# Attention gates of the first two row blocks as bf16 parts, made by GpSimd and VectorE, in a fused attention and routed-mixture kernel

## The chip, the cores and the metric

The kernel runs on one core of one Trainium2 chip. The metric is device time in microseconds (us), and smaller is better. Three runs of the kernel before took 287.94, 531.36 and 285.32 us, with a median of 287.94 us. The execution that the profiler recorded took 286.6 us; its span, from the first instruction to the last, is 284.8 us.

## The reference

The input x has 8 sequences of 512 rows of 256 numbers. A first layer computes causal attention scores of the rotated projections q and k; for every row it keeps only one number, the sum of the exponentials, `o`. That number goes through a tiny two-layer network, the **gate**: `relu(o * fc1_w + fc1_b)` has 16 values, and `fc2_w` (256 x 16) with `fc2_b` turns them into 256. The result is added to x and normalised to x1.

A second layer is a top-3 mixture of 12 experts:

```
xa = x1 @ P_w.T
C1, C2, C3 = top-3 softmax weights of xa @ U1.T, xa @ U2.T, xa @ U3.T
h  = gelu(sum_e C1[:, e] * (x1 @ W1[e].T))
y  = sum_e C2[:, e] * (h @ W2[e].T) + C3 @ b2
out = layernorm(x1 + y)
```

## The kernel before, in words

**Tiling.** The 4096 rows are 32 tiles of 128 rows. A tile mixes 16 rows of each of the 8 sequences. Four tiles are a group, so there are 8 groups (0 to 7); two groups are one block T of 128 positions, so there are 4 blocks. The attention is done in 8 chunks c = 0 to 7; chunk c holds block T = c // 2 of four sequences. Groups 2T and 2T+1 need the sums of block T.

**Three stages.** (1) The chunk loop: for each chunk, TensorE makes four fp32 projections (`project`, line 914), ScalarE copies each out of PSUM (`qk_copy`), VectorE rotates them (`rope`, lines 1279 and 1285), TensorE makes the scores and ScalarE the exponentials (`exps`). Work for the first groups is mixed in by hand through `early_aux`: the gate's product `fc`, its addition to x (`fc_add`), the statistics (`norm_stats`), scale and shift of the norm (`norm_scale`, on GpSimd), the normalised rows (`normed`, on ScalarE), their transposes and the router. (2) A middle part written out by hand: tile 0 goes through all 12 experts, tiles 1 to 3 through the chosen ones. (3) The steady loop over i = 4 to 33: first mixture of tile i, second mixture of tile i-2.

**Weights.** The expert weights are split into two fp16 parts. ScalarE and VectorE split the first experts (`w_high`, `w_low`). GpSimd splits the other 16 in 16 pieces (`w_piece`: lines 464, 466, 467), one after the other, from chunk 4 on. The first piece waits for the scales of the weights (`scale_done`) and for `fc2_spread`, the copies of the gate's second weight matrix, since it overwrites the buffer `wtmp` from which they are made. Between pieces GpSimd runs `norm_scale(0)` (before piece 0), `norm_scale(1)` (before piece 5), and the routing weights (`chosen_exps`, `weights_of`; before piece 9). Behind piece 14 comes `bias_add(0, 0)` (line 500), for which the second mixture of tile 0 waits.

**Gates.** For blocks 0 and 1, TensorE spreads `o` over 32 partitions with an fp32 transpose (`gate_spread`, after chunks 1 to 4), ScalarE applies scale, bias and relu (`gate_relu`), and `fc` is an fp32 product. For blocks 2 and 3, GpSimd computes the gate with rows on partitions and cuts it into six bf16 parts (`gate_parts`, seven linked operations), TensorE transposes them (`gate_transpose`), ScalarE copies them (`gate_copy`), and `fc` is a bf16 product against `fc2s`, the six stacked copies of the weights (`fc2_spread`, six transfers issued on the SP queue in chunk 5, each followed by one for b2).

**Order.** Each engine runs its list strictly in the order written. Buffers: two PSUM banks for projections, four for expert products, one (`ROWS`) for gate and bias rows, one (`XPOSE`) shared by the transposes of x1, C3 and the gates.

## Time and profile before

| | us |
|---|---|
| profiled execution | 286.6 |
| its span | 284.8 |
| TensorE busy in the span | 259.5 (91%) |
| VectorE busy | 214.8 (75%) |
| GpSimd busy | 180.3 (63%) |
| ScalarE busy | 175.0 (61%) |
| runs, median of 3 | 287.94 |

The shares are averages over three stages with different limits. The chunk loop takes up to about 84 us, the middle part up to about 130 us, the steady loop the rest. Which engine sets the pace has to be read stage by stage, in the chain of waits.

### The profile page before, as it was taken

What the parts mean: (1) busy time and instruction counts of PE and PEld (TensorE: products, weight loads), DVE (VectorE), ACT (ScalarE), POOL (GpSimd) and SP (SyncE); (2) the same over time, 40 slices, a digit from 0 to 9 for tenths busy, and PEclk for the clock granted to TensorE, in tenths of its full rate; (3) what the DMA queues carried; (4) which work ended last, traced back from release to release, by engine and by line L of the source; (5) the groups of instructions that cost most, each with busy time, mean ns of one, the idle gap of its engine ahead of it and who ended that gap; (6) DMA issues with size and microseconds to landing.
All of it is one profiled execution on the core that took longest, in us unless ns stands there. A gap on an engine that the chain in (4) does not pass through costs nothing.

```text
span 284.8 us, 6483 instructions
## 1 busy us (share of the span) xinstructions
PE 259.5 (91%) x2016; PEld 191.6 (67%) x2016; DVE 214.8 (75%) x668; ACT 175.0 (61%) x376; POOL 180.3 (63%) x367
## 2 busy tenths in 40 slices
PE   7999999997997878799899998998998999999980
PEld 5444455453455666678688897897897898887960
DVE  0359869779969938848898899899897877765671
ACT  2235966665763632816958957867878858655541
POOL 2640005999989998727785775685774864855552
PEclk9999999999999999959999999999999999999997
DMA  7999994997000000000001001001011010100112
GB/s 226 393 380 359 155 213 73 211 136 92 0 3 0 0 3 0 0 21 1 22 22 33 26 20 39 21 20 41 18 32 29 18 39 18 41 20 24 36 37 60
DMA packets 19546, 20.51 MB, mean 72 GB/s; under 512 B 1643, under 2 KB 18870, under 8 KB 18998
## 3 DMA queue, kind: packets, MB, share of 16 engines
q1 hardware_dynamic: 18518, 19.14, 28.4%
q10 hardware_dynamic: 992, 0.93, 1.1%
q8 instruction: 18, 0.29, 0.5%
q14 instruction: 18, 0.15, 0.2%
HBM read 15.78 MB, written 4.19 MB: 70 GB/s over the span
## 4 chain that ended last, share of the span: by engine, by line
PE 48%; POOL 20%; ACT 8%; DVE 7%; issue 6%; SPq 5%; DMA 3%; POOLq 0%; DVEq 0%; ACTq 0%
PE bank L1110 33%; PE bank L914 8%; POOL W L467 7%; POOL wtmp L464 5%; POOL W L466 4%; DVE early L1526 3%; DMA early<-in_xT 2%; PE bank L1190 2%; SPq L372 2%; ACT early L723 2%; SPq L400 1%; SPq L367 1%; PE bank L989 1%; ACT L702 1%; SPq L399 1%
## 5 line engine op out<-in xcount | busy, mean ns | idle before, releaser
L1110 PE MATMUL bank<-W,early 128*128 (+1 forms) x630 | 77.2, 277 | 4.8 <-ACT early L780 1.8
L1110 PE MATMUL bank<-W,x1T 128*128 (+1 forms) x630 | 75.0, 273 | 4.0 <-issue 2.1
L1110 PEld LDWEIGHTS bank<-W,early 128*128 128x128 f16 x630 | 61.4, 99 | 15.0 <-ACT early L780 2.6
L1110 PEld LDWEIGHTS bank<-W,x1T 128*128 128x128 f16 x630 | 60.3, 98 | 13.8 <-issue 4.5
L914 PE MATMUL bank<-early,wqk 128*128 128x512 f32 x128 | 60.3, 602 | 1.0 <-DMA early<-in_xT 1.0
L1526 DVE SCALAR_TENSOR_TENSOR early<-bank,Csel,early 128x256 f32<-128x256 f32 x95 | 45.7, 482 | 15.3 <-ACT early L780 5.4
L588 POOL TENSOR_TENSOR early<-early 128x256 f32<-128x256 f32 x29 | 21.0, 725 | 30.8 <-DVE early L1526 28.2
L658 ACT ACTIVATE qk<-bank 128x512 bf16<-128x512 f32 x32 | 19.0, 595 | 31.3 <-PE bank L914 31.2
L914 PEld LDWEIGHTS bank<-early,wqk 128*128 128x128 f32 x128 | 22.3, 190 | 21.2 <-issue 20.5
L785 ACT ACTIVATE early<-early 128x256 f32<-128x256 f32 x32 | 13.3, 417 | 35.1 <-DVE early L1526 35.0
L1279 DVE TENSOR_TENSOR xturn<-qk,turn 128x2048 bf16<-128x2048 bf16 x16 | 21.1, 1320 | 15.9 <-ACT qk L658 15.9
L1526 DVE SCALAR_TENSOR_TENSOR early<-bank,Csel,xs 128x256 f32<-128x256 f32 x31 | 14.8, 479 | 11.5 <-PE bank L1110 10.9
L827 ACT ACTIVATE early<-bank,ipow 128x256 f16<-128x256 f32 x32 | 15.0, 469 | 10.8 <-PE bank L1190 10.7
L840 ACT ACTIVATE early<-early,shift,rstd 128x256 f32<-128x256 f32 x32 | 18.8, 588 | 4.4 <-POOL shift L596 4.4
L467 POOL TENSOR_TENSOR W<-wtmp,W 128x512 f16<-128x512 f32 x16 | 20.3, 1269 | 1.4
L710 ACT ACTIVATE x<-xs,shift,rstd 128x256 f32<-128x256 f32 x32 | 17.4, 594 | 5.9 <-POOL shift L495 5.8
L492 POOL TENSOR_SCALAR ve<-mv 128x4 f32<-128x4 f32 x8 | 2.8, 352 | 28.0 <-DVE mv L1359 27.5
L500 POOL TENSOR_TENSOR xs<-early,x 128x512 f32<-128x512 f32 x16 | 20.3, 1269 | 0.0
L595 POOL TENSOR_TENSOR rstd<-ve,minus_half 128x1 f32<-128x1 f32 x32 | 18.0, 561 | 2.7
L666 ACT ACTIVATE expd<-bank 128x128 bf16<-128x128 f32 (+3 forms) x32 | 13.6, 435 | 8.4 <-PE bank L929 8.4
L1566 DVE SCALAR_TENSOR_TENSOR early<-bank,ipow,early 128x256 f16<-128x256 f32 x32 | 14.6, 457 | 5.1 <-ACT early L827 5.0
L464 POOL TENSOR_SCALAR wtmp<-W,scale 128x512 f32<-128x512 f32 x16 | 16.2, 1014 | 1.7 <-DMA fc2s<-wtmp 1.7
(139 smaller groups left out, 453.7 us busy)
## 6 DMA issues: line engine op xcount, KB each, us to landing
early<-in_xT SPq DMA_DIRECT2D x16, 256.0 KB, 7.4
xs<-in_x SPq DMA_DIRECT2D x32, 128.0 KB, 7.4
out<-early SPq DMA_DIRECT2D x32, 128.0 KB
W<-in_w1T SPq DMA_DIRECT2D x1, 2048.0 KB, 12.2
W<-in_w2T SPq DMA_DIRECT2D x1, 2048.0 KB, 12.9
W<-in_w1T SPq DMA_DIRECT2D x1, 1024.0 KB, 7.7
W<-in_w2T SPq DMA_DIRECT2D x1, 1024.0 KB, 14.6
wqk<-in_wqkT ACTq DMA_DIRECT2D x1, 512.0 KB, 3.7
```

Of the source, the lines that this page charges most:

```text
L464: link(pool.tensor_scalar(wtmp[:, n % 2, :], Wf[:, WS * m + e + 2, :], scale[:, 1 + m:2 + m], 0.0, ALU.mult, ALU.add))
L467: pool.tensor_tensor(W[:, m, e + 1, 1, :], wtmp[:, n % 2, :], W[:, m, e + 1, 0, :], ALU.subtract)\
L500: pool.tensor_tensor(xs[:, t:t + 2, :].rearrange("p t d -> p (t d)"), brows[:, h, :], x1[:, g % 3, 2 * h:2 * h + 2, :].rearrange("p t d -> ...
L588: pool.tensor_tensor(y[:, t % 4, :], y[:, t % 4, :], part[:, t % 2, :], ALU.add).then_inc(late_added, 1)
L595: link(pool.tensor_tensor(rstd2[:, p:p + 1], ve2[:, p:p + 1], minus_half[:, 0:1], ALU.pow))
L658: act.activation(qk[:, c % 2, g, :, :].rearrange("p s n -> p (s n)"), bank[PROJ[n % 2]][:, :], ACT.Copy)\
L710: n = act.activation(x1[:, g % 3, t, :], xs[:, GT * g + t, :], ACT.Identity, bias=shift[:, g % 2, t:t + 1], scale=rstd[:, g % 2, t:t + 1])
L840: act.activation(y[:, t % 4, :], y[:, t % 4, :], ACT.Identity, bias=shift2[:, p:p + 1], scale=rstd2[:, p:p + 1]).then_inc(y_done, 1)
L914: mm = pe.matmul(bank[PROJ[n % 2]][:, :], wqk[:, k, g, :], xTb[:, c % 4, k, :, :].rearrange("p s n -> p (s n)"), start=(k == 0), stop=(k = ...
L1110: mm = pe.matmul(where[:, 0:DIM], lhs(hx, c), w, start=(k == 0), stop=(k == 5))
L1279: link(dve.tensor_tensor(xturn[:, :, :, :, :], src, turns, ALU.mult))
L1526: dve.scalar_tensor_tensor(sums, bank[place[n]][:, 0:DIM], c, before, ALU.mult, ALU.add)\
```

## The change

Blocks 0 and 1 get their gates in six bf16 parts as well. Block 0's parts are made by GpSimd in chunk 2 and block 1's by VectorE at the head of chunk 5. `gate_spread`, `gate_relu`, the fp32 matrix `fc2w` and its transfer go. `fc2s` is spread in chunk 4, ahead of chunk 5's load. In chunk 3 the steps of the first gate product and its addition move to after the transposes of the weights' maxima, on TensorE and VectorE. `norm_scale(0)` moves behind piece 0 of the weights; the split of C3 and the selection for group 0 move from chunk 7 to chunk 6. In the middle part a product of tile 1 and an addition change places, and the second mixture of tile 0 takes its first four experts in the opposite order. In the steady loop the expert numbers are loaded earlier, and of the first mixture of a group's first tile one or two products (three for group 1) stand between the two bias products. Small changes of buffers and semaphores are left out.

```diff
--- before.py
+++ after.py
...
@@ -326,6 +320,10 @@
+        def dense_expert(m, j):
+            return NB - 1 - j if m and j < NB else j
@@ -386,13 +384,12 @@
             load_chunk(3)
-            sp.dma_start(fc2w[:, :], fc2[0:2 * PAD, :]).then_inc(ld_fc2, 16)
             load_rows(0)
                     load_rows(c // 2 - 1)
-                if c == 5:
+                if c == 4:
                     sp.wait_ge(fc2_split, 1)
@@ -471,8 +468,8 @@
                 pool.wait_ge(exp_done, NSEQ * (T + 1))
-                wait(pool, hgT_done, T - 2)
-                if T == 2:
+                wait(pool, hgT_done, T)
+                if T == 0:
                     pool.wait_ge(gwb_done, 1)
@@ -565,20 +562,21 @@
                         continue
-                    if (c, j) == (3, 3):
+                    if (c, j) == (2, 3):
+                        gate_parts(0)
+                    if (c, j) == (4, 1):
                         norm_scale(0)
                         weights_of(0)
+                    if (c, j) == (6, 2):
+                        C3_split(0)
+                        select_of(0)
                     if c >= 4:
                         piece += 1
-                    if (c, j) == (NCH - 1, 0):
-                        C3_split(0)
-                    if (c, j) == (NCH - 1, 2):
-                        select_of(0)
             bias_add(0, 0)
@@ -675,16 +673,9 @@
-            def gate_relu(c):
-                T, b = c // 2, SPC * (c % 2)
-                act.wait_ge(gate_done, c + 1)
-                act.activation(hgf[PAD * T:PAD * (T + 1), :, b:b + SPC, :].rearrange("p u s r -> p s u r"),
-                               bank[HGT][0:PAD, :].rearrange("p (s u r) -> p s u r", s=SPC, r=RPS), ACT.Relu,
-                               bias=gatew[0:PAD, 1:2], scale=gatew[0:PAD, 0:1]).then_inc(gate_copied, 1)
             def gate_copy(T):
-                act.wait_ge(hgT_done, T - 1)
-                act.activation(hgT[0:NP * NI, T - 2, :, :, :].rearrange("p u s r -> p s u r"),
+                act.wait_ge(hgT_done, T + 1)
+                act.activation(hgT[0:NP * NI, T, :, :, :].rearrange("p u s r -> p s u r"),
                                bank[XPOSE][0:NP * NI, :].bitcast(BF16).rearrange("p (s u r) -> p s u r", s=NSEQ, r=RPS),
@@ -747,15 +738,15 @@
                     normed(3, 0)
-                if (s, pos) == (0, 1):
-                    if group(k):
-                        bias_copy(k, 0)
+                if (s, pos) == (0, 1) and group(k):
+                    bias_copy(k, 0)
                     if k == 1:
-                        final(1)
+                        begin(GT)
                     if routed(k + 1):
                         exp_route(k + 1)
-                    if group(k):
-                        bias_copy(k, 1)
+                    if k > 1:
+                        begin(GT * k)
+                    bias_copy(k, 1)
                 if (s, pos) == (1, 1):
@@ -802,13 +793,13 @@
                 qk_copy(c, 2)
+                if c in (3, 6):
+                    gate_copy(c // 6)
                 if c:
                 qk_copy(c, 3)
-                if 1 <= c <= 4:
-                    gate_relu(c - 1)
                 early_aux(c, 2, early)
@@ -842,10 +833,10 @@
             begin(0)
+            exps(NCH - 1, 0)
             w_high(NB + 2)
-            exps(NCH - 1, 0)
+            exps(NCH - 1, 1)
             w_high(NB + 3)
-            exps(NCH - 1, 1)
             gelu(0)
@@ -876,8 +867,11 @@
                 if i < NT:
-                    begin(i)
+                    if s:
+                        begin(i)
                     gelu(i)
+                if i == GT:
+                    final(1)
                 if late(i - 3):
@@ -929,19 +923,10 @@
-            def gate_spread(c):
-                T, b = c // 2, SPC * (c % 2)
-                pe.wait_ge(exp_done, SPC * (c + 1))
-                wait(pe, gate_copied, c)
-                for s in range(SPC):
-                    tr = pe.transpose(bank[HGT][0:PAD, P * s:P * (s + 1)],
-                                      o[:, T, b + s:b + s + 1].to_broadcast([P, PAD]), identf[:, :])
-                tr.then_inc(gate_done, 1)
             def gate_transpose(T):
-                pe.wait_ge(hgp_done, T - 1)
+                pe.wait_ge(hgp_done, T + 1)
                 wait(pe, hgT_copied, begun["gate"])
-                pe.wait_ge(x1lo_done, begun["x1T"])
+                wait(pe, x1lo_done, begun["x1T"])
                 wait(pe, C3T_copied, begun["C3T"])
@@ -972,21 +957,16 @@
                 if g == 0 and h == 0:
-                    pe.wait_ge(ld_fc2, 16)
-                if T == 2 and g % 2 == 0 and h == 0:
                     pe.wait_ge(fc2_spread, 16 * NP)
-                if h == 0 and T < 2:
-                    pe.wait_ge(gate_copied, 2 * (T + 1))
-                if h == 0 and T >= 2:
-                    pe.wait_ge(hgT_copied, T - 1)
+                if h == 0:
+                    pe.wait_ge(hgT_copied, T + 1)
                 wait(pe, bias_copied, begun["bias"])
                     u = (GT * g + t) % 8
-                    lhs, rhs = (hgf[PAD * T:PAD * (T + 1), u, :, :], fc2w[PAD * T:PAD * (T + 1), :]) if T < 2 else \
-                        (hgT[0:NP * NI, T - 2, u, :, :], fc2s[:, :])
-                    mm = pe.matmul(bank[ROWS][:, t % 2 * DIM:(t % 2 + 1) * DIM], lhs.rearrange("p b r -> p (b r)"), rhs,
+                    mm = pe.matmul(bank[ROWS][:, t % 2 * DIM:(t % 2 + 1) * DIM],
+                                   hgT[0:NP * NI, T, u, :, :].rearrange("p b r -> p (b r)"), fc2s[:, :],
                                    start=True, stop=True)
@@ -1059,7 +1039,7 @@
                         x1_transpose(k + 1, 1)
-                if (s, pos) == (1, 0) and group(k + 1):
+                if (s, pos) == (1, 1) and group(k + 1):
                     route_logits(k + 1)
@@ -1075,11 +1055,12 @@
                         bias(k, 0)
-                    if between(k):
-                        routed_first(GT * k)
-                    if later(k + 2):
-                        x1_transpose(k + 2, 0)
-                    if group(k):
+                        if k == 1:
+                            routed_first(GT, range(TOPK))
+                        if later(k + 2):
+                            x1_transpose(k + 2, 0)
+                        if k > 1:
+                            routed_first(GT * k, range(ahead(k)))
                         bias(k, 1)
@@ -1095,8 +1076,8 @@
-            def between(k):
-                return k in (1, NG - 2, NG - 1)
+            def ahead(k):
+                return TOPK if k == 1 else 1 if later(k + 2) else 2
@@ -1117,7 +1098,7 @@
                         pe.wait_ge(acc_begun if act else slot_added, count)
-                    e = j + 1 if t == 0 else held_ids[t // GT][REC * m + j]
+                    e = dense_expert(m, j) + 1 if t == 0 else held_ids[t // GT][REC * m + j]
                     products(bank[place[n]], lhs, m, e).then_inc(slot_done, 1)
@@ -1136,8 +1117,11 @@
                     gate_rows()
-                early_aux(c, 0, early)
+                if c != 3:
+                    early_aux(c, 0, early)
                 project(c, 1)
+                if c == 3:
+                    gate_transpose(0)
                 if c == 0:
@@ -1148,20 +1132,22 @@
                 project(c, 2)
-                early_aux(c, 2, early)
+                if c != 3:
+                    early_aux(c, 2, early)
+                if c == 6:
+                    gate_transpose(1)
                 if c == NCH - 1:
                 if c == 3:
-                    pe.wait_ge(gwb_done, 1)
                     peak_transpose()
+                    early_aux(c, 0, early)
                 project(c, 3)
                     peak_spread()
+                    early_aux(c, 2, early)
                 early_aux(c, 3, early)
-                if 1 <= c <= 4:
-                    gate_spread(c - 1)
@@ -1175,8 +1161,7 @@
             first(range(4, 6))
-            pe.wait_ge(gate_copied, 4)
-            pe.wait_ge(ids_done, 1)
+            load_ids(0)
             scores(NCH - 1, 0)
@@ -1194,10 +1179,8 @@
-            def routed_first(t):
-                if t % GT == 0 or t == 1:
-                    load_ids(t // GT)
-                mixture(t, 0, lambda hx, c: x1T[:, t, hx, c, :], range(TOPK))
+            def routed_first(t, js=range(TOPK)):
+                mixture(t, 0, lambda hx, c: x1T[:, t, hx, c, :], js)
@@ -1205,8 +1188,10 @@
             route_logits(1)
+            pe.wait_ge(wlo_done, NM * NB - 1)
+            second(0, range(0, NB - 1))
             pe.wait_ge(wlo_done, NM * NB)
-            second(0, range(0, NB))
+            second(0, range(NB - 1, NB))
             pe.wait_ge(w_split, NM * (NE - NB) - 2)
@@ -1217,10 +1202,11 @@
             fc(3, 0)
+            gate_transpose(2)
             route_count(1)
-            gate_transpose(2)
+            second(1, range(0, 1))
             fc(3, 1)
-            second(1, range(TOPK))
+            second(1, range(1, TOPK))
             h_transpose(2)
@@ -1230,11 +1216,13 @@
                 second(i - 2, range(TOPK))
+                if s == 0 and i < NT:
+                    load_ids(k)
                 if i <= NT:
                 aux(k, s, 1)
-                if i < NT and (s or not between(k)):
-                    routed_first(i)
+                if i < NT:
+                    routed_first(i, range(0 if s else ahead(k), TOPK))
@@ -1269,6 +1257,21 @@
+            def gate_parts(T):
+                dve.wait_ge(exp_done, NSEQ * (T + 1))
+                dve.wait_ge(hgT_done, T)
+                w, b = (gwb[:, n, :].unsqueeze(1).to_broadcast([P, NSEQ, NI]) for n in range(2))
+                f = hg[:, :, :].unsqueeze(2)
+                link(dve.tensor_tensor(hg[:, :, :], o[:, T, :].unsqueeze(2).to_broadcast([P, NSEQ, NI]), w, ALU.mult))
+                link(dve.tensor_tensor(hg[:, :, :], hg[:, :, :], b, ALU.add))
+                link(dve.tensor_scalar(hg[:, :, :], hg[:, :, :], 0.0, None, ALU.max))
+                link(dve.tensor_copy(hgp[:, :, 0:3, :], f.to_broadcast([P, NSEQ, 3, NI])))
+                link(dve.tensor_tensor(hg[:, :, :], hg[:, :, :], hgp[:, :, 0, :], ALU.subtract))
+                link(dve.tensor_copy(hgp[:, :, 3:5, :], f.to_broadcast([P, NSEQ, 2, NI])))
+                dve.tensor_tensor(hgp[:, :, 5, :], hg[:, :, :], hgp[:, :, 3, :], ALU.subtract).then_inc(hgp_done, 1)
...
@@ -1486,8 +1490,11 @@
             for c in range(NCH):
+                if c == 5:
+                    gate_parts(1)
                 early_aux(c, 0, early)
-                early_aux(c, 1, early)
+                if c != 3:
+                    early_aux(c, 1, early)
                 if c == 4:
@@ -1505,11 +1512,11 @@
                     peak_pow()
+                    early_aux(c, 1, early)
                 if c in (4, 5):
                 if c == NCH - 1:
-                    w_low(NB + 1)
                     break
@@ -1520,7 +1527,7 @@
                 n = slot[t, m, j]
-                e = j + 1
+                e = dense_expert(m, j) + 1
                 c = C[:, 0, m, e:e + 1] if t == 0 else Csel[:, t, m, j:j + 1]
@@ -1572,14 +1579,15 @@
             first_mixture(0, (4,))
-            w_low(NB + 2)
+            w_low(NB + 1)
             first_mixture(0, (5,))
             first_mixture(0, (6, 7))
-            w_low(NB + 3)
+            w_low(NB + 2)
             fc_add(2, 1)
             norm_stats(2)
+            w_low(NB + 3)
             h_low(0)
@@ -1591,9 +1599,9 @@
             route_mask(1)
+            fc_add(3, 0)
             first_mixture(2)
             route_sums(1)
-            fc_add(3, 0)
             route_ids(1)
```

## Rows read from the trace of the kernel before

**Rows 1.** The chain of waits, 49 to 108 us: start, us, what ended last.
```profile
49.28 0.90 POOL wtmp L464
...
106.10 1.24 POOL xs L500
107.36 0.49 DVE early L1526
```
**Rows 2.** Windows: us, busy of PE, PEld, DVE, ACT, POOL; granted clock, DMA share, GB/s.
```profile
67.30:84.70 17.40, 17.10 (x69) 7.97 (x66) 14.59 (x56) 11.39 (x30) 15.87 (x19) 1.00 0.10 13
...
160.00:200.00 40.00, 38.29 (x390) 33.38 (x388) 36.16 (x140) 30.24 (x64) 27.24 (x71) 1.00 0.10 28
```
**Rows 3.** The timeline of the SP queue: start, us, issue, tensors, count.
```profile
16.93 6.96 SPq L389 DMA_DIRECT2D fc2w<-in_fc  x1
27.87 1.94 SPq L367 DMA_DIRECT2D early<-in_xT  x2
39.66 0.71 SPq L399 DMA_DIRECT2D fc2s<-wtmp  x1
```
**Rows 4.** The timeline of GpSimd: start, us, line, operation [idle before, releaser].
```profile
52.43 1.67 POOL L464 TENSOR_SCALAR wtmp<-W,scale 128x512 f32<-128x512 f32 x1
...
66.13 0.24 POOL L492 TENSOR_SCALAR ve<-mv 128x4 f32<-128x4 f32 x1
...
109.99 0.23 POOL L492 TENSOR_SCALAR ve<-mv 128x4 f32<-128x4 f32 x1
...
111.72 0.20 POOL L495 TENSOR_TENSOR shift<-shift,rstd 128x4 f32<-128x4 f32 x1
```
**Rows 5.** The timeline of VectorE, 46 to 66 us.
```profile
46.75 0.17 DVE L1319 TENSOR_SCALAR scale<-ipow 128x3 f32<-128x3 f32 x1
...
51.81 1.73 DVE L1279 TENSOR_TENSOR xturn<-qk,turn 128x2048 bf16<-128x2048 bf16 x1 [1.06 <-ACT qk L658]
...
58.80 0.69 DVE L1367 TENSOR_TENSOR x1T<-bank,x1T 128x512 f16<-128x512 f32 x1 [2.55 <-ACT x1T L717]
...
65.64 0.38 DVE L1359 BATCH_NORM_AGGREGATE mv<-stats 128x2 f32<-128x6 f32 x4
```
**Rows 6.** The timelines of ScalarE and TensorE, 47 to 52 us.
```profile
47.74 1.10 ACT L710 ACTIVATE x<-xs,shift,rstd 128x256 f32<-128x256 f32 x2
...
50.98 0.60 PE L1001 MATMUL bank<-identf,x 128*128 128x128 f32 x4
...
51.85 1.88 PE L914 MATMUL bank<-early,wqk 128*128 128x512 f32 x4
```
**Rows 7.** Instructions by source line: ns min/median/max, first and last start in us.
```profile
L1383 DVE TENSOR_TENSOR dz<-zs,top x8: 308/309/1059, 70.7 to 239.4; 128x144 f32<-128x144 f32 x8
...
L989 PE MATMUL bank<-fc2w,hgf x32: 374/374/762, 33.3 to 122.3; 32*128 32x256 f32 x32
...
L989 PE MATMUL bank<-fc2s,hgT x16: 270/274/283, 129.8 to 203.2; 102*128 102x256 bf16 x16
```
**Rows 8.** Windows of 1 us, columns as in Rows 2.
```profile
118.00:119.00 1.00, 0.48 (x7) 0.14 (x5) 1.00 (x4) 1.00 (x1) 0.35 (x2) 1.00 0.00 0
...
121.00:122.00 1.00, 1.00 (x3) 0.81 (x4) 0.93 (x5) 0.53 (x2) 0.79 (x4) 0.50 0.00 0
```
**Rows 9.** The timeline of TensorE, 120 to 127 us.
```profile
120.84 2.04 PE L989 MATMUL bank<-fc2w,hgf 32*128 32x256 f32 x4 [1.20 <-DVE xs L1349]
122.82 4.02 PE L1110 MATMUL bank<-W,early 128*128 x18
```
**Rows 10.** The timelines of TensorE and ScalarE at the start of group 2.
```profile
157.21 2.15 PE L1110 MATMUL bank<-W,x1T 128*128 x18 [0.40 <-issue]
...
161.17 0.38 PE L1190 MATMUL bank<-identf,early 128*128 128x128 f32 x2
...
160.09 0.42 ACT L785 ACTIVATE early<-early 128x256 f32<-128x256 f32 x1
```
**Rows 11.** Waits of TensorE, 123 to 284 us: total, times, longest.
```profile
PE bank L1110 <- ACT early L780: 1.8, 3, 0.9
```

10 lines of the change are left out of this document (3 added, 7 removed).

## The prediction

> **What bounds the kernel now.** I read the chain of waits first, then the windows, then the timelines of single engines. From 49.28 to 107.36 us the chain lies on GpSimd: the 16 pieces of the weights, with other work between them, then the addition of bias rows (line 500), for which VectorE's first sum of the second mixture waits [rows 1]. Beside it TensorE is nearly full in the loop (17.10 of 17.40 us), but it doesn't end last there [rows 2]. In the steady loop TensorE sets the pace (38.29 of 40 us), with VectorE close behind (36.16) [rows 2]. So a microsecond saved on TensorE counts after about 107 us; before, only what moves GpSimd's chain counts. The profiled execution took 286.6 us, its span 284.8; the sum below is made against these. The median shown is 287.94, 0.5% more. About 2%, 5.7 us, is what a measurement of this kernel tells from no change.
>
> **Gate products and spreads, in the loop.** An fp32 product call is four matmuls of 0.374 us at least in the record, a bf16 one two of 0.274 [rows 7]; they overlap, and from start to next start the calls cost about 1.1 and 0.3, so 0.8 is saved per call. Six of the eight calls lie before 107 us. They, the four spreads and the four relus are worth nothing: GpSimd's chain covers them. If that cover were gone they would be worth 5 us.
>
> **The weight copies for the gate, earlier on SP.** The six transfers (and six for b2) now follow chunk 4's load, whose issue ends at 29.8 us, and the first product waits for all six. Before, from the first issue (39.66) to the start of piece 0, which waited for them (49.28), took 9.6 us [rows 1, 3]. From 29.8 that gives 39.4. They are issued behind a full queue, as the transfer for the old fp32 weights was, which held SP for 6.96 us [rows 3]; so they may land up to 7 us later. I take 40.5, nearer to the first row, which is the same transfer. Chunk 5's load moves behind 12 issues and still has 10 us to land before 51.85 [rows 6]: nothing. Block 0's parts on GpSimd lie in an idle stretch: nothing.
>
> **Scales 1.7 us later.** The first additions move behind the maxima, and the second product now stands behind the fourth projection of chunk 3. VectorE's addition, statistics and rotation stand ahead of the scales, so they end at 48.6 us and not at 46.92 [rows 5]. I estimate 1.7, one fp32 projection (line 914: 1.88 for four matmuls [rows 6]) less slack; the bounds are 0 and 3.
>
> **First norm behind piece 0.** Piece 0 can't begin before the scales: 48.6. It took 3.15 (49.28 to 52.43) [rows 1, 4], so it ends at 51.8. `norm_scale(0)` takes 1.93 with VectorE quiet (109.99 to 111.92) [rows 4], so it ends at 53.7. ScalarE began the normalised rows at 47.74 [rows 6]: now 53.7, and in its list everything waits behind them: a weight split, the copies of projections 2 and 3, more exponentials. TensorE's transposes start at 54.8 instead of 50.98 [rows 6], chunk 5's projections about 4 us late. Of SP nothing waits. The last copy of chunk 4 ends at 57.3, so VectorE's rotation starts at 57.4 instead of 51.81 [rows 5]: **+5.6**. GpSimd itself loses nothing yet.
>
> **Block 1's parts on VectorE.** Seven linked operations at the head of chunk 5. The nearest row is a fp32 operation on 128x144: 0.309 alone, 1.059 once, at 70.7 us, beside the pieces [rows 7]. Lower bound 7 x 0.31 = 2.2; upper 7 x 1.06 plus links = 7.7. I take 5.5: four operations with two tensor inputs at 1.06, three with one at 0.31, and links. VectorE had 2.55 idle there, waiting for ScalarE [rows 5]; the late rotation makes it the last, so this idle time goes. Its statistics for group 1 ended at 66.02 [rows 5]: 66.0 + 5.6 + 5.5 - 2.55 = 74.6, less 1.5, since GpSimd by then stands and no longer slows VectorE: 73.1.
>
> **GpSimd's chain: +6.7.** `norm_scale(1)` began at 66.13, just after these statistics [rows 4], and eleven pieces are queued behind it. It begins at 73.2 and takes 1.93 where it took 2.4. Line 500 moves by 6.7. Bounds: 2.5 (scales on time, piece 0 at its shortest, the parts 2.2) and 9.
>
> **The early split of C3 and selection, expert order, early numbers: nothing** before 107 us. They let TensorE reach the second mixture at about 104, where it makes four products and stops: its four banks are full, and VectorE waits for line 500 until 114. **Clock: +2.0.** In the profile TensorE, busy 0.48 us of the microsecond from 118, had a granted clock of 0.50 (1.2 of 2.4 GHz) at 121 [rows 8], and 18 matmuls took 4.02 us against 2.15 [rows 9, 10]: 0.6 per expert. The new idle stretch is over 4 us; three or four experts run slow. Bounds 0 and 3.4.
>
> **The middle part behind it: -4.9.** The fp32 calls of group 3: 0.8 off the first; the wait of 1.20 for VectorE's addition goes (that addition is earlier, and a product of tile 1 fills in); the second call shrinks from 1.98 to 0.2; 18 matmuls at full clock give 1.9 [rows 9, 10]. That is 5.7; I take off 0.8 for VectorE, which then ends last. Bounds 3 and 6.
>
> **Group boundaries.** ScalarE's first product copy comes before a table load or a bias copy; TensorE waited three times for it, 1.8 in all [rows 11]: **-1.8**. In groups 2 to 5 a product fills the wait between the bias products, and the numbers are loaded early; 0.40 of the idle time there is the loading [rows 10]. But the transposes of h can't start before the gelu's end at 160.5; they started at 161.17 [rows 10]. So 0.67 each: **-2.7**. Bounds 0 and -4.7.
>
> **Sum:** 6.7 + 2.0 - 4.9 - 1.8 - 2.7 = -0.7; 286.6 - 0.7 = 285.9 us.
>
> **Rivals.** *A, the forecast:* 285.9, its own range 282.5 to 289; chance 0.40.
>
> *B, the early loss is small:* the rotation catches up, the parts take 2.2, the clock holds. 2.5 - 4.9 - 1.8 - 2.7 = -6.9: 279.7. For it: VectorE waits 2.55 in that stretch. Against it: ScalarE's list is strict. Chance 0.22.
>
> *C, slower, the weight copies in a full queue:* if their last part lands later than about 42 us, TensorE stands in front of the first gate product, with projection, scales and pieces behind it. With 5 us lost there (the hold of 6.96 less 2 of slack): 285.9 + 5 = 290.9. For it: the hold [rows 3]. Against it: the copies were issued 0.7 apart behind eight loads. Chance 0.13.
>
> *D, the boundaries give nothing,* since VectorE, busy 36.16 of 40, becomes the bound [rows 2]: 285.9 + 4.5 = 290.4. Chance 0.15.
>
> *E, every operation of block 1's parts waits for a whole operation of a piece:* 7.7 us instead of 5.5, and 2.2 more on the chain: 288.1. The row at 1.06 against 0.31 speaks for it, rotations beside pieces, 1.73 against 1.2, only mildly [rows 5, 7]. Chance 0.10. The Trainium skill, page "SBUF — State Buffer", section "SBUF: two separate sides", states this as an exclusive lock between VectorE and GpSimd, held for the whole instruction, the other fully blocked. By that rule the trace's 1.06 would be the normal case for all seven.
>
> **Range and chances.** From 279 to 291: it takes in B, C, D and E. The part of B below 280.9 is most of it: faster by over 2%, 0.22. C and D together, or a stall of TensorE in chunk 4 that also halves its clock among the fp32 projections, would pass 292.3: slower by over 2%, 0.10. The rest, 0.68, is within 2%.
>
> **What would show it.** Piece 0 starting before `norm_scale(0)`, the copies at line 710 starting at 53 to 54, idle TensorE before its first transposes; block 1's seven operations at about 0.7 us each, and GpSimd idle before its second `norm_scale` (right for A; no idle there means B). Line 500 at 112 to 114, then a clock of 0.50. The stretch from the first sum of the second mixture to tile 3's first product (107.4 to 127.8 before) about 3 us shorter. Group boundaries 0.7 shorter. I am wrong if TensorE stands before the first gate product for over 2 us (C), or if line 500 comes before 109 (B).

## The result: a little slower, where no change was forecast

The changed kernel took 289.4 us (median of 4 runs, 289.1 to 291.0): a ratio of 1.014 to the kernel before, 95% interval 1.009 to 1.019. Beside it the kernel before took 285.1, 285.3 and 287.9; a fourth run, 531.4, was slow and is left out; it is in the median of 287.94 that the opening gives. The profiled execution took 289.3 us, its span 287.4, against 286.6 and 284.8 before. The forecast was 285.9, 0.7 less than 286.6; the span grew by 2.6. The time lies inside the range, but the sign was wrong by more than the interval.

The page of the changed kernel: the span, the busy time of each engine, TensorE's granted clock in 40 slices.
```profile
span 287.4 us, 6466 instructions
...
PE 252.3 (88%) x2000; PEld 188.3 (66%) x2000; DVE 219.3 (76%) x675; ACT 173.0 (60%) x374; POOL 183.4 (64%) x374
...
PEclk9999999979999999599999999999999999999996
```
TensorE has 7.2 us less to do than before and the span is 2.6 us longer: most of what went was covered, the waits that came were not. The row PEclk is the clock that TensorE was granted, in tenths of full speed. By windows of 1 us it was halved (0.50) from 57.6 to 60.7 us and from 115.6 to 122.1 us; the last digit is the end, where TensorE has nothing left. "To stand" below means that an engine waits.

The chain of waits of the changed kernel answers to [rows 1] (start, us, what ended last; "issue" is time without a wait that shows):
```profile
49.53 0.71 POOL wtmp L461
...
53.87 1.06 POOL rstd L490
55.53 1.09 ACT x L701 x2
...
58.96 1.32 DVE xturn L1282
...
64.33 1.36 DVE hgp L1270
...
75.03 1.05 POOL rstd L490
...
114.95 1.23 POOL xs L497
116.83 2.72 PE bank L1091 x12
```
Before, one engine carried this stretch. Now the chain leaves GpSimd behind piece 0, goes over ScalarE and VectorE, through block 1's parts (line 1270), and comes back at 75 us. Lines 461 to 464 are the pieces, 497 the addition of bias rows.

The timelines of the same kernel, GpSimd and then VectorE, TensorE and the copies, answer to [rows 4, 5, 6]; in brackets stands the idle time ahead and what ended it:
```profile
49.53 0.70 POOL L461 TENSOR_SCALAR wtmp<-W,scale 128x512 f32<-128x512 f32 x1 [14.33 <-DVE scale L1322]
...
53.23 0.56 POOL L489 TENSOR_SCALAR ve<-mv 128x4 f32<-128x4 f32 x1
...
62.28 1.26 POOL L461 TENSOR_SCALAR wtmp<-W,scale 128x512 f32<-128x512 f32 x1
63.60 0.61 POOL L463 CAST W<-wtmp 128x512 f16<-128x512 f32 x1
64.30 1.16 POOL L464 TENSOR_TENSOR W<-wtmp,W 128x512 f16<-128x512 f32 x1
65.43 0.81 POOL L461 TENSOR_SCALAR wtmp<-W,scale 128x512 f32<-128x512 f32 x1
66.31 0.61 POOL L463 CAST W<-wtmp 128x512 f16<-128x512 f32 x1
67.00 1.15 POOL L464 TENSOR_TENSOR W<-wtmp,W 128x512 f16<-128x512 f32 x1
74.70 0.24 POOL L489 TENSOR_SCALAR ve<-mv 128x4 f32<-128x4 f32 x1 [6.55 <-DVE mv L1363]
...
114.91 1.26 POOL L497 TENSOR_TENSOR xs<-early,x 128x512 f32<-128x512 f32 x1
```
```profile
49.19 0.17 DVE L1322 TENSOR_SCALAR scale<-ipow 128x3 f32<-128x3 f32 x1
...
55.53 1.09 ACT L701 ACTIVATE x<-xs,shift,rstd 128x256 f32<-128x256 f32 x2 [5.72 <-POOL shift L492]
...
56.68 0.66 PE L981 MATMUL bank<-identf,x 128*128 128x128 f32 x4 [3.37 <-ACT x L701]
57.86 3.35 PE L908 MATMUL bank<-early,wqk 128*128 128x512 f32 x4 [0.53 <-ACT qk L656]
...
58.96 1.31 DVE L1282 TENSOR_TENSOR xturn<-qk,turn 128x2048 bf16<-128x2048 bf16 x1 [0.33 <-ACT qk L656]
...
62.77 0.29 DVE L1267 TENSOR_TENSOR hg<-o,gwb 128x136 f32<-128x136 f32 x1
63.09 0.59 DVE L1268 TENSOR_TENSOR hg<-hg,gwb 128x136 f32<-128x136 f32 x1
63.71 0.58 DVE L1269 TENSOR_SCALAR hg<-hg 128x136 f32<-128x136 f32 x1
64.33 1.35 DVE L1270 CAST hgp<-hg 128x408 bf16<-128x408 f32 x1
65.72 0.67 DVE L1271 TENSOR_TENSOR hg<-hg,hgp 128x136 f32<-128x136 f32 x1
66.42 0.65 DVE L1272 CAST hgp<-hg 128x272 bf16<-128x272 f32 x1
67.11 1.20 DVE L1273 TENSOR_TENSOR hgp<-hg,hgp 128x136 bf16<-128x136 f32 x1
...
68.97 0.39 PE L968 MATMUL bank<-fc2s,hgT 102*128 102x256 bf16 x2 [3.28 <-DVE xs L1353]
```
Lay the two side by side: from 63.1 on each of the last six of block 1's seven operations ends 0.1 to 0.2 us after the GpSimd operation that had started before it: 63.68 after 63.54, 64.29 after 64.21, 65.68 after 65.46, 66.39 after 66.24, 67.07 after 66.92, 68.31 after 68.15. Their ends follow GpSimd's; e3 below has the same operations where they need not wait. The first of the seven (62.77) took 0.29; there GpSimd's operation took long, 1.26 for what takes 0.69 at its shortest, so there GpSimd seems to have been the one that waited.

And TensorE's first gate product, then its stand in front of the fifth product of tile 0's second mixture:
```profile
41.27 0.39 PE L968 MATMUL bank<-fc2s,hgT 102*128 102x256 bf16 x2 [2.39 <-DMA fc2s<-wtmp]
...
116.83 2.72 PE L1091 MATMUL bank<-W,early 128*128 128x256 f16 x12 [5.40 <-DVE early L1533]
...
125.51 2.13 PE L1091 MATMUL bank<-W,x1T 128*128 x18
...
129.12 0.62 PE L934 MATMUL bank<-cb,hgp 128*102 128x128 bf16 x8 [1.27 <-DVE x1T L1371]
...
132.71 2.13 PE L1091 MATMUL bank<-W,x1T 128*128 x18
...
136.14 0.77 PE L997 MATMUL bank<-MT,x1T 128*128 128x36 f16 x24 [1.05 <-DVE x1T L1371]
...
145.64 0.44 PE L1175 MATMUL bank<-identf,early 128*128 128x128 f32 x2 [0.56 <-ACT early L776]
```
The last three marks of the table below, in the kernel before:
```profile
115.12 2.13 PE L1110 MATMUL bank<-W,x1T 128*128 x18
...
127.80 2.13 PE L1110 MATMUL bank<-W,x1T 128*128 x18
...
139.58 0.44 PE L1190 MATMUL bank<-identf,early 128*128 128x128 f32 x2 [0.24 <-ACT early L785]
```

**Where the 2.6 us are.** Four marks cut the span: VectorE's first sum of tile 0's second mixture, the first product of tile 2 and of tile 3, and the transposes of tile 4's h; "rest" is what the span has behind the last. All are starts from the timelines; the lower kernels are told of below.

| kernel | first sum | tile 2 | tile 3 | h of tile 4 | rest |
|---|---|---|---|---|---|
| before | 107.36 | 115.12 | 127.80 | 139.58 | 145.2 |
| changed | 116.20 | 125.51 | 132.71 | 145.64 | 141.8 |
| steady loop alone (e6) | 107.28 | 115.05 | 126.05 | 137.81 | 141.7 |
| and the middle's order (e11) | 107.23 | 115.01 | 123.00 | 135.14 | 141.7 |
| changed, TensorE kept busy (e7) | 116.34 | 124.12 | 131.43 | 144.26 | 141.8 |
| norm ahead, parts behind (e3) | 109.84 | 118.36 | 125.56 | 138.48 | 141.6 |

Stretch by stretch, changed against before: +8.84 up to the first sum, +1.55 to tile 2, -5.48 to tile 3, +1.15 to tile 4's h, -3.46 after it; together +2.6.

### The profile page after: what moved, and what is told of

It is laid out like the page before. It is cut to its first block, busy times and chain, and to the rows that moved or that the text cites. A ratio compares the mean times of both kernels' runs of the same rounds, so it can differ in the third digit from the quotient of the medians.

```text
span 287.4 us, 6466 instructions
## 1 busy us (share of the span) xinstructions
PE 252.3 (88%) x2000; PEld 188.3 (66%) x2000; DVE 219.3 (76%) x675; ACT 173.0 (60%) x374; POOL 183.4 (64%) x374
## 4 chain that ended last, share of the span: by engine, by line
PE 34%; POOL 16%; ACT 14%; DVE 13%; SPq 13%; issue 7%; DMA 1%; POOLq 0%; ACTq 0%; DVEq 0%
PE bank L1091 28%; POOL W L464 5%; SPq L370 3%; POOL wtmp L461 3%; POOL W L463 3%; ACT L693 3%; DVE early L1533 3%; SPq L374 2%; SPq L365 2%; ACT early L714 2%; PE bank L1175 2%; SPq L397 2%; DVE stats L1359 2%; SPq L396 2%; ACT L776 2%
## 5 line engine op out<-in xcount | busy, mean ns | idle before, releaser
L1091 PE MATMUL bank<-W,x1T 128*128 (+1 forms) x630 | 75.9, 273 | 1.4 <-DVE early L1533 1.0
L1091 PEld LDWEIGHTS bank<-W,x1T 128*128 128x128 f16 x630 | 61.0, 98 | 9.2 <-DVE early L1533 1.2
L908 PEld LDWEIGHTS bank<-early,wqk 128*128 128x128 f32 x128 | 23.1, 194 | 23.2 <-issue 22.2
L1282 DVE TENSOR_TENSOR xturn<-qk,turn 128x2048 bf16<-128x2048 bf16 x16 | 20.5, 1280 | 15.3 <-ACT qk L656 15.2
L461 POOL TENSOR_SCALAR wtmp<-W,scale 128x512 f32<-128x512 f32 x16 | 14.4, 898 | 14.3 <-DVE scale L1322 14.3
L497 POOL TENSOR_TENSOR xs<-early,x 128x512 f32<-128x512 f32 x16 | 20.3, 1270 | 0.0
L771 ACT ACTIVATE early<-bank,Csel 128x256 f32<-128x256 f32 x31 | 14.5, 468 | 1.6 <-PE bank L1091 1.3
```

Of the source, the lines that this page charges most:

```text
L461: link(pool.tensor_scalar(wtmp[:, n % 2, :], Wf[:, WS * m + e + 2, :], scale[:, 1 + m:2 + m], 0.0, ALU.mult, ALU.add))
L497: pool.tensor_tensor(xs[:, t:t + 2, :].rearrange("p t d -> p (t d)"), brows[:, h, :], x1[:, g % 3, 2 * h:2 * h + 2, :].rearrange("p t d -> ...
L908: mm = pe.matmul(bank[PROJ[n % 2]][:, :], wqk[:, k, g, :], xTb[:, c % 4, k, :, :].rearrange("p s n -> p (s n)"), start=(k == 0), stop=(k = ...
L1091: mm = pe.matmul(where[:, 0:DIM], lhs(hx, c), w, start=(k == 0), stop=(k == 5))
L1282: link(dve.tensor_tensor(xturn[:, :, :, :, :], src, turns, ALU.mult))
```

## Experiments

Each kernel ran beside the kernel before; the ratio is to that, with its 95% interval. The marks come from one profiled execution of each. "Addition" is GpSimd's first addition of bias rows (106.1 before, 114.9 changed).

**e1: the norm ahead of piece 0 again.**
```
-                    if (c, j) == (4, 1):
+                    if (c, j) == (4, 0):
                         norm_scale(0)
```


> GpSimd takes the first tiles' norm scale ahead of the first piece of W again; all else as in the changed kernel (289.4 us, 1.014 of the kernel before). Theory 1 (two causes of about equal size: the norm behind the piece, and VectorE's seven operations in front of group 1's statistics): ScalarE's first normalised rows come at 49 instead of 55.5, the rotation of chunk 4 at 52.5 instead of 58.96, GpSimd's second norm scale at 68.2 instead of 74.7, the first addition of bias rows at 108.4 instead of 114.9; no halved clock at 57 to 60; total 282.9 (0.991). Theory 2 (VectorE's operations are the whole loss, the late norm is caught up by the loop): the second norm scale stays above 73, total 288 to 289. Theory 3 (the late middle and the group boundaries hold the end, not the loop): the addition moves as in theory 1, but the last products move by less than 3: total above 286.

Measured: 285.8 us, 1.000 (0.997 to 1.003); addition 113.97. The total fell by some 4 us, the addition in the profile by only 0.9. The execution profiled took 287.9 us, as long as the longest of the ten (284.3 to 287.9), so it shows less of the gain than the median does. In it the stand for the gate's weights came first, as in the changed kernel, but chunk 3's projection behind it ran at half clock (the windows give 0.71 for 40 to 44 us), 3.47 us for what takes 1.9; later TensorE stood 4.74 for VectorE.
```profile
41.32 0.39 PE L968 MATMUL bank<-fc2s,hgT 102*128 102x256 bf16 x2 [2.58 <-DMA fc2s<-wtmp]
41.55 3.47 PE L908 MATMUL bank<-early,wqk 128*128 128x512 f32 x4
...
66.37 0.61 PE L968 MATMUL bank<-fc2s,hgT 102*128 102x256 bf16 x2 [4.74 <-DVE xs L1353]
```
So its scales came at 51.07 and not at 49.36. From the scales' end to GpSimd's second norm scale took 21.9 us against 25.3 in the changed kernel and 19.2 before: the late norm is 3.5 of the 6.1 lost there. Theory 1 holds in part, theory 2 falls; theory 3's condition did not come about.

**e2: block 1's parts behind group 1's statistics.**
```
             for c in range(NCH):
-                if c == 5:
-                    gate_parts(1)
...
                 rope(c, 1)
+                if c == 5:
+                    gate_parts(1)
```


> VectorE's seven operations on block 1's gates stand behind the statistics of group 1 and the rotation of chunk 5's keys, instead of at the head of chunk 5; the norm stays behind the piece. Theory 1: GpSimd's second norm scale at 69.2 instead of 74.7, the addition of bias rows at 109.4 instead of 114.9; TensorE, whose own list is not moved (four products of the second mixture end at 111.4), does not stand in front of its fifth product, so no halved clock there either: total 282.5 (0.989). Theory 2 (VectorE's operations only change places, and something behind them is late by as much: the exponentials' mask, GpSimd's multiplication at 90.6): the addition stays above 112, total 288 or more. Theory 3 (end held elsewhere): addition at 109.4, total above 286.

Measured: 287.2, 1.006 (1.003 to 1.009); addition 113.93. From the scales to the second norm scale 22.8 us, 2.5 less, and not 5.5: TensorE's late projections now end last. They ran at half clock (3.28 us for what takes 1.9). Behind it 1.6 were lost again, as theory 2 says: GpSimd stood 2.57 at 89.4 for the mask, which VectorE makes later.

**e3: both edits.**

> Both edits: norm ahead of the first piece, block 1's parts behind the statistics. Theory 1: the second norm scale at 66 (the pieces ahead of it end then, no idle time of GpSimd in front of it), the addition of bias rows at 106.2, as in the kernel before; TensorE stands 2 to 3 us in front of the fifth product of the second mixture; total 280 (0.980), so all of the early loss is in these two places. Theory 2 (each only uncovers the other or a third): total no better than the better of the two alone. Theory 3: addition at 106.2, but total above 286, as the kernel before.

Measured: 282.2, 0.989 (0.986 to 0.993): 1.1% faster than the kernel before. The second norm scale comes at 67.39 with no idle time ahead (18.65 from the scales), the addition at 108.55. The addition is 6.4 us earlier than in the changed kernel. From the scales' end to the addition it is 5.7 (59.8 against 65.6; before 59.1), and that is what these two places cost; the other 0.6 is the scales' own end, since the gate's weights happened to land earlier (first gate product at 40.65 behind a stand of 1.37). Theory 1 holds in the main, with the addition still 2.5 late and TensorE's stand 5.39 instead of 2 to 3; theory 2 falls. VectorE's parts show another thing (VectorE, then GpSimd, of this kernel):
```profile
69.14 0.30 DVE L1267 TENSOR_TENSOR hg<-o,gwb 128x136 f32<-128x136 f32 x1
69.47 0.30 DVE L1268 TENSOR_TENSOR hg<-hg,gwb 128x136 f32<-128x136 f32 x1
...
70.07 0.38 DVE L1270 CAST hgp<-hg 128x408 bf16<-128x408 f32 x1
...
71.19 0.58 DVE L1273 TENSOR_TENSOR hgp<-hg,hgp 128x136 bf16<-128x136 f32 x1
```
```profile
67.39 1.08 POOL L489 TENSOR_SCALAR ve<-mv 128x4 f32<-128x4 f32 x1
68.56 1.52 POOL L490 TENSOR_TENSOR rstd<-ve,minus_half 128x4 f32<-128x4 f32 x1
```
All seven took 2.6 us here, five of them while GpSimd had only operations on 4 columns, and 5.5 in the changed kernel, among the operations of the pieces.

**e4: the gate's copies first, b2's behind them** (on e3).
```
                     for k in range(NP):
                         sp.dma_start(fc2s[...]).then_inc(fc2_spread, 16)
+                    for k in range(NP):
                         sp.dma_start(b2s[...]).then_inc(b2_spread, 16)
```


> As the last, and SP issues the six copies of the gate's weights first and the six for b2 behind them, instead of in turns. Theory 1: the first gate product starts at 40 or before instead of 41.27, TensorE does not stand 2.39 us in front of it; scales end 0.8 to 1.2 earlier than 49.36, and the first piece with them; the second norm scale and the addition move by the same 0.8 to 1.2, total 279 (0.976). Rival: the scales wait for VectorE's own list, and the gain is below 0.3: total as the last. Second rival: the copies do not land earlier, because the first of them is issued at the same time and each takes its own time in a full queue: the stand stays above 1.5.

Measured: 281.4, 0.985 (0.982 to 0.989). TensorE stood 1.26 and the gate product came at 40.17, against 1.37 and 40.65 in e3. In the profile the scales moved by 0.5 and the addition by 0.3, and the interval overlaps that of e3: a gain of this size is not shown.

**e5: the addition of bias rows two pieces earlier** (on e4).
```
+                    if (c, j) == (NCH - 1, 2):
+                        bias_add(0, 0)
...
-            bias_add(0, 0)
             w_piece(piece)
```


> As the kernel with both edits and the copies in order (281.4 us, 0.985), and GpSimd adds the first bias rows two pieces earlier (before pieces 13 and 14 of 0 to 15 instead of behind them). There the rows are copied at 102 and GpSimd adds them at 108.5. Theory (the wait of VectorE and TensorE is for this one addition, not for the pieces): the addition at 103.4, VectorE's first sum of the second mixture at 104.7 instead of 109.5, TensorE's fifth product at 107.3 (it waits for piece 13, which comes 1.3 later) instead of 110.2, with a stand of 1 to 2 us instead of 3.7 to 5.4, at a full clock; the last two products wait for piece 15 at 112.5; total 278 (0.973). Rival 1: the last pieces hold TensorE as long, so the gain is under 1: total 280.5 or more. Rival 2: GpSimd waits for the copy of the rows, the pieces come 1 to 2 us later still, total no better than 281.

Measured: 281.4, 0.987 (0.982 to 0.991): no gain. The addition came at 102.77 and TensorE went on at 106.68, as the theory has it; the total of 278 did not come. The next wait took its place:
```profile
106.68 1.49 PE L1093 MATMUL bank<-W,early 128*128 128x256 f16 x12 [2.22 <-POOL W L465]
...
115.00 0.66 PE L983 MATMUL bank<-identf,x 128*128 128x128 f32 x4 [4.00 <-ACT x L703]
```
Group 2's normalised rows wait for GpSimd's norm scale behind the last piece.

**e6: the kernel before with the steady loop's part alone.** (Its edits are those of `aux`, `begin`, `ahead`, `load_ids` and the place of `final(1)` in the diff of the change.)

> The kernel before, and of the change only the steady loop's part: a group's numbers loaded one step earlier, one or two products of the next tile between the two bias products in groups 2 to 7, ScalarE's first product copy before the table load or the second bias copy, the last normalisation of tile 1 behind the gelu. The prediction's terms: 2.7 for the boundaries of groups 2 to 5 and 1.8 for those of 1, 6 and 7: 4.5 in all, so 282.0 (0.984). What the trace of the changed kernel says: 0.5 for each of groups 2 to 5, nothing for 6, 1.1 for 7 and about 0.2 for 1: 3.3 in all, 283.2 (0.988). Rival D (VectorE is the bound): 286 to 286.5 (0.998 to 1.0).

Measured: 281.2, 0.986 (0.980 to 0.992). Behind tile 4's h the span has 141.7 us, against 145.2 before: -3.5, as in every kernel with this part whose marks the table has. Rival D falls. The profile's other 1.7 lie between tile 2 and tile 3, where nothing was changed: by windows of 1 us the halved clock there lasted from 120.8 to 127.7 before and from 121.7 to 125.1 here.

**e7: TensorE kept busy in its stand** (on the changed kernel).
```
+            for _ in range(38):
+                pe.matmul(bank[XPOSE][:, 0:DIM], zeros[:, 0:P], zeros[:, :], start=True, stop=True)
             pe.wait_ge(w_split, NM * (NE - NB) - 2)
             second(0, range(NB, NB + 2))
```


> The changed kernel (289.4, 1.014), and TensorE makes 38 products of zeros (4 us in all, into a bank that nothing reads) in its stand of 5.4 us in front of the fifth product of the second mixture. Nothing is computed from them. Clock theory: the granted clock stays 1.0 behind the stand instead of 0.50 for some 6 us; the 18 matmuls of the following experts take 2.1 instead of over 3.3; tile 2's first product comes 1.5 to 2 earlier (125.5 to 123.8), and the total falls by 1.5: 287.9 (1.009). Rival (VectorE, not TensorE, sets the middle part's pace): tile 2's first product comes earlier, tile 4's does not, total 289.4. Second rival: the products of zeros outlast the stand and delay what follows: later by up to 1.

Measured: 288.3, 1.012 (1.006 to 1.018). In total this is not told apart from the changed kernel (1.014), in the trace it is: tile 2 came 7.78 behind the first sum, before 7.76, in the changed kernel 9.31, and what follows is equal within 0.1. The windows of 116 to 122 us in the changed kernel, then in this one (columns as in [rows 2]):
```profile
116.00:122.00 6.00, 5.17 (x25) 3.73 (x26) 4.96 (x22) 1.19 (x3) 5.34 (x11) 0.50 0.00 0
```
```profile
116.00:122.00 6.00, 4.22 (x38) 3.56 (x38) 5.29 (x23) 1.05 (x3) 5.34 (x11) 1.00 0.00 0
```
The halved clock costs 1.5; in the trace both rivals fall.

**e8: the gate's copies ahead of the first loads of rows** (on e5).
```
+            sp.wait_ge(fc2_split, 1)
+            for k in range(NP):
+                sp.dma_start(fc2s[...]).then_inc(fc2_spread, 16)
             load_rows(0)
```


> As the first of these four, and SP issues the six copies of the gate's weights ahead of the first eight loads of rows (at 17 us) instead of behind chunk 4's load (at 28). Theory (the first gate product waits for the last of these copies: 1.3 us in that kernel, 2.4 in the changed one): no stand in front of the first gate product, which comes at 38.9 instead of 40.2; scales and first norm 1.0 to 1.3 earlier, the pieces and the addition of bias rows by 1; total 1 us less than the first of these, 277 (0.969). Rival: the eight row loads and chunk 4's load land 3.6 later and VectorE's first addition, or chunk 4's projection, waits for them instead: no gain or a loss of up to 2.

Measured: 281.1, 0.986 (0.981 to 0.990): nothing. The wait for the transfer is gone, and 1.03 for ScalarE's copy of the gates (line 680) stands in its place; the first gate product comes at 39.85, 0.2 earlier than in e5. The rows were not late here.

**e9: VectorE's low half of group 2's rows earlier** (on the changed kernel).
```
+            x1_low(2, 0)
             row_stats(0)
             h_low(1)
-            x1_low(2, 0)
```


> The changed kernel (289.4, 1.014) with one edit in the middle part: VectorE's low half of group 2's first transposed rows (line 1371) moves ahead of tile 0's statistics and of the low half of h; it starts at 125 instead of 128.19. It is what TensorE waits for (1.27 us) in front of the spread of block 2's gates, the wait that took the place of the 1.20 of the kernel before. Order theory: the wait of 1.27 goes, all of the middle part behind it comes 1.0 to 1.2 earlier and stays so: transposes of h behind tile 4 at 144.5 instead of 145.64, total 288.3 (1.010). Bound theory (VectorE and ScalarE have no room in the middle part, whichever operation comes first): the wait moves to another place (the first product of tile 1's second mixture, which waits for the low half of h, or the 1.05 in front of the logits), the transposes stay within 0.3 of 145.6, total 289.4.

Measured: 289.2, 1.012 (1.006 to 1.018). The wait of 1.27 became 0.31 for the mask, that of 1.05 stayed, and tile 2 to tile 4's h took 19.5 instead of 20.1. Between the two theories; the total can't tell.

**e10: group 2's norm scale ahead of the last two pieces** (on e8).
```
+                    if (c, j) == (NCH - 1, 3):
+                        norm_scale(2)
...
-            norm_scale(2)
             gate_parts(2)
```


> The kernel with norm ahead, parts behind, copies and bias addition early (281.1, 0.9855), and GpSimd takes the norm scale of group 2 ahead of the last two pieces instead of behind them (its statistics are done at 101.5). TensorE stood 3.98 us in front of the transposes of group 2's first rows (at 115.0) and went on at half clock for 3 us. Theory (this wait is the next one on the chain): the norm scale at 106.6, the transposes at 111.0 without a wait, the last two products of tile 0 at 113.7 (they wait for the last piece), full clock; tile 2's first product at 115.7 instead of 118.5; total 2 to 2.8 less: 278.7 (0.977). Rival (VectorE and ScalarE set the middle part): tile 2's product earlier as said, but the transposes of h behind tile 4 stay within 0.5 of 137.6, total 281.

Measured: 279.6, 0.979 (0.974 to 0.984). The stand of 4 us is gone, 2.44 for the last piece are left, tile 2 at 115.80. In the trace the theory holds: tile 2 comes 2.7 earlier than in e8. At tile 3 it is 1.5, since tile 2's products ran at half clock behind the stand of 2.44. The total is 1.5 us lower, of the 2.0 to 2.8 expected, and its interval overlaps that of e8.

**e11: steady loop and the middle's order, gates in fp32 as before** (on e6).
```
             fc(3, 0)
-            route_count(1)
             gate_transpose(2)
+            route_count(1)
+            second(1, range(0, 1))
             fc(3, 1)
-            second(1, range(TOPK))
+            second(1, range(1, TOPK))
...
+            fc_add(3, 0)
             first_mixture(2)
             route_sums(1)
-            fc_add(3, 0)
```


> The kernel before with the steady loop's part (281.2, 0.986) and of the middle part only the order: VectorE adds the gate products of group 3's first half ahead of tile 2's mixture, TensorE spreads block 2's gates before it counts, and a product of tile 1 stands between the two gate calls, which stay in fp32. The prediction's term said that the wait of 1.20 goes and 18 matmuls run at full clock: 3.1 less 0.8 for VectorE; so 2.3 less: 279 (0.978), first product of tile 3 at 125.5 instead of 127.8. Rival, from the trace of the changed kernel (the wait comes back as one for VectorE's low half of the transposed rows, in front of the spread, 1.27, and in front of the logits, 1.05): under 0.7 less, 280.7 or more.

Measured: 278.9, 0.976 (0.972 to 0.980). TensorE's granted clock stays at 1.00 in the middle part. From tile 2 to tile 4's h it took 20.13 us: exactly what the changed kernel took, whose group 3 has bf16 products (before 24.46, e6 22.76). So the middle's gain is the order; the shorter products add nothing. Of these 4.3 us, 2.6 are the step from e6, which lacks only this order; the other 1.7 e6 had already, by a shorter stretch of halved clock and without an edit there.
```profile
119.96 1.12 PE L992 MATMUL bank<-fc2w,hgf 32*128 32x256 f32 x4
...
125.64 0.77 PE L1020 MATMUL bank<-MT,x1T 128*128 128x36 f16 x24 [0.29 <-DVE x1T L1374]
```
The products of 1.12 are still there, and the wait for VectorE's low half is 0.29 where the changed kernel has 1.05, and the one of 1.27 is gone: what bf16 saves, TensorE stands.

**e12: e10 with e9's edit.**

> The second of these four, with the first one's edit too (VectorE's low half of the transposed rows ahead of tile 0's statistics). If both theories hold: another 0.5 to 1.0 less than the second: 278 (0.974). If VectorE has no room in the middle part: the same as the second within 0.3.

Measured: 279.5, 0.978 (0.974 to 0.982): the same as e10, and tile 2 to tile 4's h took 20.4 in both: the second theory.

**f1 and f3: e11 with the twelve copies elsewhere.** f1 puts the gate's six ahead of the first rows, as in e8; f3 puts all twelve where the change has them, `if c == 4` instead of `if c == 5`.

> The kernel before with the steady loop's part and the middle's order (278.9, 0.976), and SP issues the six copies of the gate's weights ahead of the first loads of rows, and not behind chunk 5's. There GpSimd stood 2.1 us for them in front of its first piece. Theory (GpSimd's chain ends last up to the addition of bias rows): the first piece at 47.5 instead of 49.5, the addition at 104.9 (the rows are copied then) instead of 106.0, total 1 less, 278 (0.973). Rival (TensorE's own list is as late: it stood only 0.20 and 0.81 there): total within 0.3 of 278.9.

> The kernel before with the steady loop's part and the middle's order (278.9, 0.976), and the twelve copies for the gate and b2 behind chunk 4's load, as in the changed kernel, not behind chunk 5's and the second rows. Theory (GpSimd's wait of 2.1 us for them ends last up to the addition of bias rows): the first piece at 47.3 instead of 49.5, the addition at 104.9 (the rows are copied then) instead of 106.0, VectorE's first additions not later, total 0.5 to 1 less: 278.2 (0.973). Rival (TensorE's own list is as late): within 0.3 of 278.9. Second rival (chunk 5's load, now behind the copies, lands late): 280 or more.

Measured: f1 280.4, 0.980 (0.976 to 0.985); f3 278.4, 0.973 (0.968 to 0.978). In f1 the rows came late: VectorE's first addition waited 5.00 us for them (2.40 in e11) and the addition of bias rows came 1.9 later. In f3 it came at 105.58, 0.4 earlier, though the first piece began 1.85 earlier (47.38 against 49.23): GpSimd was never idle, but its pieces up to the second norm scale took 18.25 us instead of 16.84. So a piece that starts earlier is not done earlier by as much. f3 is the fastest kernel here, 2.7% below the kernel before; its step from e11 is within the intervals.

**f2: e3 with five of the seven parts left out.**

> The kernel with norm ahead and block 1's parts behind the statistics (282.2, 0.989), and five of the seven operations on block 1's gates are left out (its gates are then not what they should be), so VectorE has about 2 us less to do at 69. Theory P (the 2.45 us by which the addition of bias rows is still late are these operations): it comes at 106.5 instead of 108.5, total 280.5. Theory S (they are hidden now; the late scales, 49.4 instead of 46.9, and the pieces that follow them are the rest): it stays at 108.2 to 108.6, total 282.

With these gates rows choose more experts than the lists hold, and the kernel adds its long path over all experts; so its 1,283 us say nothing and only the trace up to the addition is read. The scales came at 50.34 (half clock behind the stand for the gate's weights again), so the addition came at 109.81, where neither theory has it. The stretches can be compared: 18.66 to the second norm scale and 40.81 on to the addition; e3 has 18.65 and 41.16. That is theory S: once moved, the five operations cost 0.35 at most.

## Why the prediction was wrong

**The steps that failed** are two terms of the sum, GpSimd's chain and the middle part. In the first the mechanism and the places were those named and the size was off; in the second a part of the mechanism, the shorter products, counted for nothing.

*GpSimd's chain: forecast +6.7, measured +8.8.* The scales' end moved 2.4, not 1.7: TensorE stood 2.39 in front of the first gate product, the condition that the prediction set for rival C ("over 2 us"), though it cost 0.7 more than forecast here and not C's 5. I took 40.5 for that product, it came at 41.27. Piece 0 with the norm scale took 6.0 (49.53 to ScalarE's 55.53) where I had 5.1: 3.70 for the piece (forecast 3.15) and 2.30 for the norm scale (1.93, from a row with VectorE quiet). ScalarE's normalised rows came at 55.5 (forecast 53.7), the transposes 56.68 (54.8), the rotation 58.96 (57.4). The parts on VectorE took 5.5 as forecast, and the subtraction of slack was right: from rotation to norm scale 15.7, forecast 15.8. So the whole error of 1.5 at the second norm scale came in ahead of ScalarE. Another 0.6 came in behind it: I had taken off 0.4 for a shorter norm scale, which took 2.4 as before, and the rest of the chain took 0.3 longer. That a stand of TensorE (3.37 at 56 us) halves its clock among the projections I had only in the tail; it happened, one took 3.35 for 1.88, but it lies inside the 15.7.

*The middle part: forecast -4.9 and ScalarE's copy at group 1 about -0.9, measured -4.3 together.* Up to tile 3 it was -5.5. Then 1.15 were given back, most of it in a wait for VectorE's low half of the rows (1.05). The copy at group 1 was worth nothing: from tile 3 to tile 4's h e6 took 11.76 us and the kernel before 11.78, with waits of 0.45 and 0.58 for ScalarE where it had 0.92 and 0.24. The fp32 calls of group 3 were the wrong entry: the 0.8 us that bf16 takes off each call counted for nothing (e11 keeps both calls, and is as fast); of the 1.8 for the second call, 0.9 came with the full clock (1.06 from start to next start in e11, 1.98 before). The wait of 1.20 did not go either, it came back as 1.27 for another operation of VectorE. What is real is the order, and the clock that it keeps; how much of the clock's part is the order's is open, since e6 got 1.7 of it without an edit.

**What held.** The halved clock: forecast 2.0, measured 1.55 by stretch and 1.53 by e7. Group boundaries: forecast -2.7 and, for groups 6 and 7, about -0.9; measured -3.46, e6 -3.5. From the transposes of h to the next, the boundaries of groups 2 to 5 became 0.5 to 0.65 shorter each (forecast 0.67), that of group 6 not at all, that of group 7 by 1.2. The fp32 products in the loop: worth nothing, as said. The sum's error is 2.1 - 0.45 + 1.5 + 0.1 = 3.3, the 2.6 measured less the -0.7 forecast; the errors hardly cancel, and the time stayed inside the range because the range is wide. The medians lie further apart, by 4.1 us.

**The rivals.** B and D fell. C was right in its place and not in its price. E's mechanism fits too, and its price was too high: six of the seven operations did wait for a whole operation of a piece, but those last 0.6 to 1.2 us, so the seven took 5.5 and not 7.7. This is what the exclusive lock of the Trainium skill, page "SBUF — State Buffer", section "SBUF: two separate sides", would do; the ends in the two timelines agree with it, and e3 shows the same operations at 2.6 where there is little to wait for. The page sets a condition that the prediction left out: it names VectorE operations with two SBUF inputs or in a 2-port performance mode. Four of the seven have two inputs; the maximum and the two casts have one, and they waited too (0.58, 1.35 and 0.65 us), which the page allows only in such a mode, and no run here shows the mode. I had the right sum from the wrong picture, four slow operations and three quick ones.

**Open:** of the 2.5 by which e3's addition is still late, 1.2 lie in GpSimd's first pieces (49.34 to 67.39 instead of 49.28 to 66.13), and 1.2 behind them, of which f2 gives at most 0.35 to the parts. The first 1.2 need not be due to the gates: f3, with fp32 gates, took 18.25 there. Which operations of VectorE hold GpSimd wasn't tried. Nor was the piece of the change that started it all taken alone: bf16 gates of block 0 with everything else as before.

## What to carry to other kernels

When products are moved off an engine that is not last, cost the moved work's inputs (weights that must land, a norm behind a piece) where they enter the chain, not the products. A wait for a semaphore hides the next wait behind it: list both before taking the first one away. Take a mixed change apart: here half of it (e11) was worth 2.4% and the other half cost more. Even with its places mended, the kernel with all gates in bf16 took 279.5 (e12); with fp32 gates and the twelve copies moved it took 278.4 (f3), so no run here shows a gain from the bf16 gates themselves.

## What the runs showed of the hardware

- Granted clock: TensorE stands in front of the first gate product in seven kernels whose code up to there is the same. Behind stands of 1.94 (f2), 1.99 (e9) and 2.58 us (e1) the clock was halved for about 3 us, behind 1.37 (e3), 2.09 (e2), 2.39 (changed) and 2.40 (e7) it stayed at 1.00. Behind a stand of 2.44 at 114 it was halved in e10 and not in e12. Behind 3.37 and 5.40 (changed kernel) it was halved. So one and the same stand can cost more in one execution than in the next: in f2 and e1 the scales came 1.0 and 1.7 us later than in the changed kernel. The halved stretch differs for equal code, 6.8 us before and 3.4 in e6, which moved the span by 1.7 us.
- Three of VectorE's fp32 operations on 128x136 (lines 1268, 1269, 1271) took 0.23 to 0.30 us in e3 and 0.58 to 0.67 in the changed kernel, the cast to 408 columns 0.38 and 1.35: the wait for GpSimd stands in the records as duration, not as idle time.
- A piece on GpSimd took 2.6 us at its shortest and up to 4.7 among VectorE's operations (e3's second), from start to next start.
